# A third one-hot product in each step of the first phase, and radial transfers issued ahead of the coefficients

## The reference

```python
# first layer, for each edge e
w = silu(silu(edge_radial @ W1 + b1) @ W2 + b2) @ W3 + b3    # 256 numbers per edge
m = tensor_product(h[src], edge_sh, w)                       # 32 numbers per edge
out = h_self + segment_sum(m, dst) / 4
x = layernorm(x + out)
# then three layers of
msg = sum over 8 corners of basis * (x @ W)[src, corner]
x = bn(leaky(segment_sum(msg, dst) / degree + x @ R + b) + x)
```

## Time and profile before

| | us |
|---|---|
| median of 3 runs (13393.53 to 13436.19) | 13394.38 |
| the profiled execution | 13392.0 |
| its span | 13390.2 |
| PE busy | 12688.5 (95%) |
| DVE busy | 10615.8 (79%) |
| POOL busy | 9934.2 (74%) |
| ACT busy | 8016.0 (60%) |

### The profile page before, as it was taken

How to read it: one execution, slowest core, us unless ns; L and a number is a source line. 1 busy time by engine, 2 the same in 40 slices (tenths; PEclk the granted TensorE clock), 3 DMA queues, 4 the chain that set the end, 5 groups by cost and what they waited for, 6 DMA issues and landing times.

```text
span 13390.2 us, 249718 instructions
## 1 busy us (share of the span) xinstructions
PE 12688.5 (95%) x78543; PEld 9414.6 (70%) x78543; DVE 10615.8 (79%) x17019; ACT 8016.0 (60%) x14968; POOL 9934.2 (74%) x10386
## 2 busy tenths in 40 slices
PE   6789999999989999999989999999998999999997
PEld 2334444444458888888868888888886888888886
DVE  7888888888877777777777777777777777777777
ACT  1123333333347777777757777777775777777775
POOL 7777777777767777777767777777776777777775
PEclk8899999999989999999999999999998999999998
DMA  2111111111111111111111111111111111111111
GB/s 53 22 26 25 25 26 26 26 26 25 25 42 35 33 35 35 33 34 35 33 44 33 34 33 35 35 33 35 33 34 42 34 33 35 35 33 35 35 33 44
DMA packets 961392, 443.09 MB, mean 33 GB/s; under 512 B 683695, under 2 KB 913996, under 8 KB 961040
## 3 DMA queue, kind: packets, MB, share of 16 engines
q0 software_dynamic: 334464, 184.18, 9.3%
q1 hardware_dynamic: 455800, 228.17, 6.4%
q10 hardware_dynamic: 171032, 29.61, 1.2%
HBM read 404.28 MB, written 36.84 MB: 33 GB/s over the span
## 4 chain that ended last, share of the span: by engine, by line
POOL 41%; PE 40%; issue 14%; DVE 3%; DMA 1%; POOLq 0%; SPq 0%; ACT 0%; DVEq 0%; ACTq 0%
POOL xg L675 41%; PE ps L1850 25%; PE ps L1951 9%; PE ps L1975 2%; PE ps L1787 1%; PE ps L1875 0%; DVE big L1383 0%; PE ps L1840 0%; PE ps L1934 0%; PE ps L1816 0%; POOL big L675 0%; DMA xg<-in_x,idx 0%; PE ps L1835 0%; DMA big<-in_rad 0%; PE ps L1928 0%
## 5 line engine op out<-in xcount | busy, mean ns | idle before, releaser
L675 POOL DMA_INDIRECT xg<-x_rows,idx x7329 | 6982.1, 953 | 2305.3 <-issue 2229.4
L1850 PE MATMUL ps<-x_high,row_hot 128*128 128x512 f32 (+1 forms) x15440 | 5756.8, 376 | 35.8 <-DVE big L1590 16.7
L1850 PE MATMUL ps<-x_low,row_hot 128*128 128x512 f32 (+1 forms) x15440 | 5483.2, 374 | 0.0
L970 ACT ACTIVATE row_hot<-row_of,window_ids 128x256 fp32r<-128x256 f32 (+1 forms) x8232 | 3194.9, 469 | 1290.9 <-PE ps L1850 1290.9
L675 POOL DMA_INDIRECT xg<-in_x,idx x2969 | 2862.5, 964 | 922.4 <-issue 900.9
L1850 PEld LDWEIGHTS ps<-x_high,row_hot 128*128 128x128 f32 x15440 | 2905.4, 188 | 873.0 <-issue 312.2
L1850 PEld LDWEIGHTS ps<-x_low,row_hot 128*128 128x128 f32 x15440 | 2908.9, 188 | 537.0
L1590 DVE TENSOR_TENSOR big<-ps,col_hot 128x512 f32<-128x512 f32 x2058 | 1414.2, 687 | 1584.9 <-PE ps L1850 994.9
L1951 PE MATMUL ps<-big 128*128 128x128 f32 x18816 | 2397.7, 281 | 9.3 <-DVE big L1602 9.3
L1951 PEld LDWEIGHTS ps<-big 128*128 128x128 f32 x18816 | 2203.7, 193 | 11.1 <-DVE big L1602 11.1
L975 ACT ACTIVATE row_hot<-row_hot 128x1792 fp32r<-128x1792 f32 (+1 forms) x1176 | 1777.3, 1511 | 90.3
(11 more groups left out here) (168 smaller groups left out, 8995.6 us busy)
## 6 DMA issues: line engine op xcount, KB each, us to landing
row_of<-pick_rows SPq DMA_DIRECT2D x294, 448.0 KB
xg<-x_rows,idx POOLq DMA_INDIRECT x7329
xg<-in_x,idx POOLq DMA_INDIRECT x2969
carry<-carry_items SPq DMA_DIRECT2D x392, 48.0 KB
agg_rows<-rts ACTq DMA_DIRECT2D x294, 64.0 KB
meta<-in_coord_t SPq DMA_DIRECT2D x294, 48.0 KB
big<-in_rad SPq DMA_DIRECT2D x784, 16.0 KB
row_of<-pick_rows SPq DMA_DIRECT2D x79, 128.0 KB
```

The source lines that it names most:

```text
L675: return nc.gpsimd.indirect_dma_start(out=dst_tile, out_offset=None, in_=table, in_offset=bass.IndirectOffsetOnAxis(ap=index, axis=0))
L970: far = nc.scalar.activation(hot[:, :, b, :], row_of[:, par, ks.start:ks.stop, :], ACT.Abs, bias=window_ids[:, b:b + 1], scale=-1.0)
L1850: tr = nc.tensor.matmul(ps[:, bank, 0:wide], hot[:, b, :], x_part[:, b * ROW:b * ROW + wide], start=(b == begin and n == 0), stop=(b == WB ...
```

## The change

The tiles of a step whose rows come from products are 15, 23 and 31 where they were 23 and 31. GpSimd gathers 29 tiles of a step in place of 30. TensorE makes the products behind the turns 0, 3 and 6 in place of 1 and 5, and VectorE selects them behind quads 2, 5 and 7 in place of 4 and 7. ScalarE forms two one-hot matrices in the turn 3 and one in the turn 0, where it formed one in each. SyncE issues the radial transfers of a step ahead of the coefficients.

```diff
-FIRST_PICKS = slice(4, 7, 2)
-FIRST_AHEAD = 1
-FIRST_PRODUCTS = {1: 0, 5: 1}
-FIRST_SELECTS = {4: 0, 7: 1}
+FIRST_PICKS = slice(2, 7, 2)
+FIRST_AHEAD = 2
+FIRST_PRODUCTS = {0: 0, 3: 1, 6: 2}
+FIRST_SELECTS = {2: 0, 5: 1, 7: 2}
...
                 if more:
                     load_indices(0, i + 1, 1 - par, twice, late)
-                load_meta(i, par, 0 if early and i < 2 else i - 1, sh_table, 5, META, in_frame)
                 load_radials(i, 0)
                 load_radials(i, 1)
+                load_meta(i, par, 0 if early and i < 2 else i - 1, sh_table, 5, META, in_frame)
                 load_carry(i - 1, 1 - par, 0 if early and i < 3 else i - 2)
```

## The result

The changed kernel takes 13596.83 us (median of 4 runs, 13591.38 to 13598.79), the kernel before 13393.99 beside it: a ratio of 1.0147 as estimated from all runs (the two medians alone give 1.0151), with a 95% interval from 1.0133 to 1.0161. It is 203 us slower, 1.5%; 13,589 was forecast, which is 195 us slower.

A forecast was written before the change was run, and what follows sets the result against it. Gathers were taken to bound the kernel at 37.92 us a step. TensorE's 38.01 + 1.46 + 0.92 = 40.39 us is 2.47 more, 195 us in 79 steps: 13,589 us, 8-in-10 range 13,470 to 13,690.

The forecast's parts named there:

- Gathers set the pace before: GpSimd: 30 gathers make the 37.92 us step; one fewer gives 36.65, 1.26 us less, if others keep up.
- bare step: TensorE without any wait: 35.02 us a step before, plus 2.99 for the added product, 38.01 us.
- The order on SyncE: Radial transfers 1.2 us sooner, coefficients and later issues 3.63 us later but covered by other work; nothing taken.
- Wait at quad 0: Step's end: the last select delays features, reduction and quad 0's product; TensorE stands 1.15 us, 1.46 on the mean.
- Wait at quad 6: Quads 1 to 6: two selects but one product between; TensorE waits 0.92 us for VectorE's product of quad 6.
- fit into TensorE's slack: Rival: the product fits TensorE's 2.90 us of waiting and slow clock, GpSimd stays the bound; 13,294 us, chance 0.06.
- TensorE alone: Rival: no new wait for VectorE, TensorE's 38.01 us sets the step; 13,401 us, chance 0.10.
- The clock rival: Rival: waits at quad 0 also lower TensorE's clock, 1.72 us more a step; 13,725 us, chance 0.12.
- the steps before 18: Sign: the steps before the products begin are as long as before.
- The waits of L1303 for L1850: Sign: VectorE's select waits for a product, some 3 us once a step; hardly any wait would refute the forecast.
- GpSimd's wait: Sign: GpSimd waits for features (L1344) some 3.7 us a step.
- the wait of L1875 for L1383: Sign: TensorE's sums wait for VectorE's product twice a step, above 1 us at quad 0, under 1 at quad 6.

The follow-up runs named there:

- the run with both edits: Changed kernel with the second select behind quad 6 and the third held until behind quad 1 of the next step; 13410.12 us, ratio 1.0012.
- the faster version: Changed kernel with products behind turns 1, 5 and the last first layer, selects behind quads 4, 7 and next step's quad 1; 13323.37 us, ratio 0.9948.

## Why the prediction was right

**Gathers set the pace before, and one is worth 1.26 us a step.** Shown: without it the kernel takes 102 us less in 79 steps, 1.29 us each.

**The product costs TensorE 2.99 us, and its bare step is 38.01.** Shown by the run with the product behind quad 5, 38.01 us a step. In the changed kernel's own order on TensorE it is 37.94, as the run with both edits shows, 0.1 less: the degrees, now with a product behind them, take 2033.02 to 2033.53, 0.51 us, against 0.61.

**The order on SyncE is worth nothing.** Shown from both sides, in the changed kernel and in the kernel before. The reason given, that TensorE "only waits less", was wrong: it waits as long, since its wait is what the pace leaves over.

**Wait at quad 0, forecast 1.46 us on the mean.** From the turning (L1798) to the bias (L1835) takes 2041.79 to 2044.59 = 2.80 us; in the faster version, where nothing is late, 2015.49 to 2017.34 = 1.85. That is 0.95 us. In the step before, which has the loop's end, 2001.04 to 2004.46 = 3.42 makes 1.57; the mean is 1.26. The term was 0.2 too large: the features at this place take 1.45 us (2038.10 to 2039.55), not 1.57, because what follows them is a reduction that needn't wait for them, and the select starts 0.11 us after quad 7's sums (2036.54 to 2036.65), not 0.20. The mechanism was shown by holding the select.

**Wait at quad 6, forecast 0.92 us.** From the second layer's start to the sums it takes 2028.44 to 2030.74 = 2.30 us, against 2012.09 to 2013.14 = 1.05 where nothing waits: 1.25. The term was 0.3 too small. The prediction let TensorE wait for the product of quad 6, which ended at 2029.99, and start 0.24 later. It waits for the reduction behind it (L1287, from 2029.91), which frees the PSUM bank that the sums go to, and starts 0.75 later: that is the releaser the profile names. The kernel's code has it so: all pairs of quads are summed in one bank (`SUMS`), and at every even quad `item_sums` waits for the reduction of the pair before (`pair_out`) besides the product. The chain is one instruction longer than was summed.

The step was forecast at 40.39 and is 40.4. That the sum is so close is partly luck, since the two waits were off by 0.2 and 0.3 in opposite directions and the bare step by 0.1.

**The rivals and the signs.** The product did not fit into TensorE's slack: the weight loads are busy 1194.18 / 2500 = 48%, and yet of the versions with three products only the one whose product stands in a real pause of the queue gains. The rule of the Trainium skill (Perfetto Trace Analysis, Identifying the Most-Contended Engine) judges TensorE's headroom by the work done against the peak and by the busy share of the weight loads; by that share TensorE would be half free. Here the trace disagrees: with every wait for VectorE gone, steps still took 37.94 to 38.01 us, the bare work read from start to start, although the gathers needed only 36.6. TensorE alone did not set the step either, as long as the selects stood where the change put them. The clock rival did not come: with waits of up to 1.4 us in every step the granted clock is 1.00. Of the signs, the steps before 18 are as long as before (the degrees of step 18 start at 820.6 us against 823.5). The waits of L1303 for L1850 came 62 times in 62 steps with 3.7 us each, where some 3 were said; GpSimd's wait was 4.3 us a step, where 3.7 was said. One sign did not come as stated: the wait of L1875 for L1383 was to come twice in a step, at quad 6 under 1 us. It comes once, at quad 0 (65.7 / 62 = 1.06 us); at quad 6 the wait is for L1287, and with 72.7 / 62 = 1.17 us it is over 1.

## What to carry to other kernels

Where engines hand work round in a loop, a piece moved to an engine with time to spare pays for that engine's own work plus every wait that its place makes for the others. So ask of each new instruction what is queued behind it on its engine, and whether the thing it waits for ends before that engine has run out of other work. A wait that recurs every step may only be the slack against the slowest engine: shortening what it waits for moves it, and the slack is better spent by putting work into a real pause. Read an engine's bare work from the start-to-start time of a step without waits, and test the chains apart by moving one consumer at a time.

## What was not expected of the hardware

A radial transfer that starts 1.1 us sooner left TensorE's wait for it as it was, 135.3 us against 132.7. In the kernel before, the granted clock behind a wait of 2.69 us was 0.57, mostly the lower level, and over the stretch 0.97. In the changed kernel, which waits in every step but never above 1.4 us at a time, it was 1.00 over the stretch; with one gather less, where the waits reach 1.8 us, it was 1.00 too. The degrees took 0.51 us with a product behind them and 0.61 with the sums of a quad behind them.
